# A four-layer transformer kernel: where the causal mask products stand in the transposed scores, and which head pairs run together

## The reference

```python
h = norm(x) * (1 + scale1) + shift1
x = x + gate1 * (softmax(q @ k.T / sqrt(16)) @ v @ wo + bo)     # 16 heads of 16 features
h = norm(x) * (1 + scale2) + shift2
x = x + gate2 * (act(h @ w1 + b1) @ w2 + b2)                    # 1024 hidden features
```

## Time and profile before

| | |
|---|---|
| median of 3 runs | 2475.57 us (2473.37 to 2478.87) |
| profiled execution, its own time | 2480.4 us |
| its span | 2478.5 us |
| TensorE busy | 2306.8 us (93%), 20776 products |
| VectorE, ScalarE, GpSimd busy | 66%, 51%, 44% |
| mean granted clock of TensorE | 0.982 |

### The profile page before, as it was taken

The page is one execution under the profiler, slowest core; times in us unless marked ns, Lnnn a source line. Parts: engine busy times, 40 slices in busy tenths (PEclk is TensorE's granted clock), DMA queues, the critical chain, the costliest instruction groups (busy, mean ns, idle before and its releaser), DMA issues.

```text
span 2478.5 us, 63608 instructions
## 1 busy us (share of the span) xinstructions
PE 2306.8 (93%) x20776; PEld 1908.5 (77%) x20776; DVE 1646.9 (66%) x3820; ACT 1255.5 (51%) x2624; POOL 1084.0 (44%) x1319
## 2 busy tenths in 40 slices
PE   6699999999999999999999999999999999999997
PEld 5477778877778778877777777777778787887876
DVE  3566676666665565556766676667777777677763
ACT  0366655566655554555666655566543433434332
POOL 1244444544544444444554444445534344343433
PEclk9799999999999999999999999999999999999988
DMA  6222121122211211122222211122221111111110
GB/s 211 84 67 69 63 61 61 59 71 80 90 63 57 66 59 51 61 69 78 86 79 67 68 57 58 60 70 84 64 82 45 63 51 50 65 42 60 52 53 14
DMA packets 165535, 166.66 MB, mean 67 GB/s; under 512 B 29392, under 2 KB 144976, under 8 KB 165424
## 3 DMA queue, kind: packets, MB, share of 16 engines
q1 hardware_dynamic: 165424, 165.21, 20.8%
HBM read 58.99 MB, written 4.39 MB: 26 GB/s over the span
## 4 chain that ended last, share of the span: by engine, by line
PE 47%; issue 20%; POOL 15%; DVE 10%; ACT 3%; SPq 1%; POOLq 1%; DMA 0%; DVEq 0%; ACTq 0%
PE B L481 20%; POOL GHl L1244 7%; PE B L581 7%; PE B L724 4%; PE B L530 4%; PE B L747 4%; PE B L506 3%; ACT PR L905 3%; DVE NEGM L976 2%; PE B L590 2%; POOL H1l L1283 2%; POOL X L1230 2%; POOL H2l L1270 1%; POOL X L1238 1%; PE B L600 1%
## 5 line engine op out<-in xcount | busy, mean ns | idle before, releaser
L905 ACT ACTIVATE PR<-B 128x512 f32<-128x512 f32 (+1 forms) x1024 | 508.4, 564 | 433.7 <-PE B L724 329.0
L1244 POOL TENSOR_TENSOR GHl<-G,GHh 128x256 fp32r<-128x256 f32 x512 | 376.5, 736 | 503.0 <-ACT GHh L878 332.1
L976 DVE TENSOR_REDUCE NEGM<-B 128x2 f32<-128x512 f32 x768 | 479.0, 683 | 78.7 <-PE B L530 78.0
L481 PE MATMUL B<-H2h,W1h 128*128 128x256 f32 x1280 | 394.5, 308 | 5.1 <-issue 3.1
L878 ACT ACTIVATE G<-B,VEC 128x256 f32<-128x256 f32 x384 | 182.1, 474 | 359.0 <-PE B L481 355.6
L481 PE MATMUL B<-H2h,W1l 128*128 128x256 f32 x1280 | 362.8, 283 | 0.0
L481 PE MATMUL B<-H2l,W1h 128*128 128x256 f32 x1280 | 362.3, 283 | 0.0
L747 PE MATMUL B<-PR,V 128*32 128x256 f32 (+1 forms) x4096 | 270.2, 383 | 62.8 <-ACT PR L905 62.1
L581 PE MATMUL B<-W2h,GHh 128*128 128x256 f32 x1024 | 299.2, 292 | 5.9 <-POOL GHl L1244 5.7
L581 PE MATMUL B<-W2l,GHh 128*128 128x256 f32 x1024 | 289.5, 283 | 0.0
L581 PE MATMUL B<-W2h,GHl 128*128 128x256 f32 x1024 | 288.7, 282 | 0.0
(11 more groups left out here) (140 smaller groups left out, 4977.1 us busy)
## 6 DMA issues: line engine op xcount, KB each, us to landing
QS<-QHL SPq DMA_DIRECT2D x768, 64.0 KB, 2.1
KS<-KHL SPq DMA_DIRECT2D x768, 64.0 KB, 2.1
GA<-gate_scratch SPq DMA_DIRECT2D x48, 256.0 KB, 3.1
GM<-gate_scratch SPq DMA_DIRECT2D x48, 256.0 KB, 3.4
RAW<-in_w SPq DMA_DIRECT2D x36, 256.0 KB, 3.9
CW<-in_cw SPq DMA_DIRECT2D x3, 1536.0 KB, 13.8
X<-in_x SPq DMA_DIRECT2D x2, 2048.0 KB, 10.2
QS<-MT SPq DMA_DIRECT2D x256, 4.0 KB
```

What stands on the lines that cost most here:

```text
L481: last = nc.tensor.matmul(dst, w[i], x[j], start=(first_k and n == 0), stop=(last_k and n == 2))
L905: nc.scalar.activation(PR[:, h % PRING].rearrange("p k q -> p (k q)")[:, 0:n], src[:, 0:n], ACT.Exp, scale=SCALE).then_inc(ac_exp, 1)
L976: last = nc.vector.tensor_reduce(NEGM[:, :, c], src, op=ALU.max, axis=AX.X, negate=True)
L1244: nc.gpsimd.tensor_tensor(GH[1][:, j % RING, :], G[:, j % RING, :], GH[0][:, j % RING, :].bitcast(F32), ALU.subtract).then_inc(po_gl, 1)
```

## The change

The mask product may now lead: it opens the accumulation in its bank (`start=True`) and the score products add to it. A new tuple `MASK_LEADS = (0, 3, 5, 6)` names the groups for which this holds. A new function takes one or more pairs, waits for the banks of all of them, then (in the causal layer, if the group leads) runs all their mask products, and then their score products. Outside `rope` pairs 0 and 1 are one group; in every step pairs 6 and 7 are one group. Where the mask leads, `pe_st` is raised by the product for k = 1.

```diff
+MASK_LEADS = (0, 3, 5, 6)
...
-                def mask(transposed, n):
+                def mask(transposed, n, leads=False):
...
-                    return nc.tensor.matmul(dst, IDENTB[:], MASK[:, transposed], start=False, stop=True,
+                    return nc.tensor.matmul(dst, IDENTB[:], MASK[:, transposed], start=leads, stop=not leads,
                                             skip_group_check=True)
...
-                def transposed_pair(p):
+                def transposed_pairs(*ps):
+
+                    for p in ps:
+                        banks_free(p)
+                    leads = ps[0] in MASK_LEADS
+                    if s.la == CAUSAL and leads:
+                        for p in ps:
+                            for h in (2 * p, 2 * p + 1):
+                                mask(1, ST_BANKS[rope][h], True)
+                    for p in ps:
+                        transposed_pair(p, leads)
+
+                def banks_free(p):
...
+                def transposed_pair(p, leads):
...
                             last = nc.tensor.matmul(B[:, banks[h], k * T:k * T + T - first], KS[b:b + ROWS, p, k * P:(k + 1) * P],
-                                                    QS[b:b + ROWS, p, first:T], start=(k == 0 or s.la != CAUSAL),
-                                                    stop=(s.la != CAUSAL), skip_group_check=(s.la == CAUSAL))
-                            if s.la != CAUSAL and k == NT - 1:
+                                                    QS[b:b + ROWS, p, first:T], start=(k == 0 and not leads or s.la != CAUSAL),
+                                                    stop=(leads and k == NT - 1 or s.la != CAUSAL),
+                                                    skip_group_check=(s.la == CAUSAL))
+                            if (s.la != CAUSAL or leads) and k == NT - 1:
                                 last.then_inc(pe_st, 1)
-                    if s.la == CAUSAL:
+                    if s.la == CAUSAL and not leads:
                         for h in (2 * p, 2 * p + 1):
                             mask(1, banks[h]).then_inc(pe_st, 1)
...
-                    transposed_pair(0)
-                    if not rope:
-                        transposed_pair(1)
+                    if rope:
+                        transposed_pairs(0)
+                    else:
+                        transposed_pairs(0, 1)
...
-                    transposed_pair(6)
-                    transposed_pair(7)
+                    transposed_pairs(6, 7)
```

More of the change, by code:

```diff
@@ L719, in transposed_pair @@
                             at_least(pe, dv_k, s.q_done)
+                def transposed_pair(p, leads):
+                    a_, banks = s.a, ST_BANKS[rope]
                     for k in range(NT):
@@ L808, in body @@
                 if s.a is not None:
-                    transposed_pair(0)
-                    if not rope:
-                        transposed_pair(1)
+                    if rope:
+                        transposed_pairs(0)
+                    else:
+                        transposed_pairs(0, 1)
                     maxima_to_rows(1)
                     if rope:
-                        transposed_pair(1)
+                        transposed_pairs(1)
                     if not rope:
                         values(0)
-                    transposed_pair(2)
+                    transposed_pairs(2)
                     if not rope:
                         values(1)
-                    transposed_pair(3)
+                    transposed_pairs(3)
                     outputs(0)
-                    transposed_pair(4)
+                    transposed_pairs(4)
                     if rope:
                         values(0)
-                        transposed_pair(5)
+                        transposed_pairs(5)
                         values(1)
```

## The result

The changed kernel is slower. In the first comparison its median is 2488.43 us (2484.45 to 2492.45, 5 runs) against 2473.37 us (2470.27 to 2478.87, 5 runs), ratio 1.0051, 95% interval 1.0035 to 1.0067. In a second, longer comparison it is 2488.38 us (12 runs) against 2476.19 us (25 runs), ratio 1.0045, interval 1.0029 to 1.0062. In microseconds the first is a loss of 13, between 9 and 17, the second a loss of 11, between 7 and 15. The prediction said 2483.6 from 2475.6, a loss of 8.0, range 2477 to 2490.

A forecast was written before the change was run, and what follows sets the result against it. Attention tails in layers 0 and 2 were taken as set by exponential 11, pair 6, four exponentials, outputs(3), next MLP. Layer 0 +6.1, layer 2 +3.5, causal -1.6 sum to +8.0: 2475.6 becomes 2483.6 us, range 2477 to 2490.

The forecast's parts named there:

- pair 6's wait in layers 0 and 2: Attention tail: pair 6 needs exponential 11 instead of 9; +0.28 us a step in layer 0, +0.23 in layer 2.
- rival 1: Causal layer: masks gain nothing, a mask behind a full-array product pays 0.21; sum +13.0, 2488.6 us; chance 0.13.
- Pair 0 waits for the maximum of head 14: Layer 0 tail start: pair 0 starts 0.27 us later, the MT copy moves by +0.10 a step.
- norm_2's wait: Layer 2: norm_2 waits 0.53 us for TOK on VectorE, untouched by the change, so pair 0's delay is absorbed.
- The leading masks: Causal layer, 16 steps: fewer array re-divisions gain 0.32 up to norm_2; net -0.10 us a step, -1.6 in sum.
- the stall of up(1): Causal tail: up(1) stalls 0.27 us on the copy VT, which takes up outputs(3) coming 0.16 later.
- Layer 3: Pairs 6 and 7: exponential 11 ends before pair 6 starts anyway, so joining them costs nothing.
- 2: Causal layer gains in full, pair 6's group not late; causal part -5.1, sum +4.5, 2480.1 us; chance 0.10.
- 3 (GpSimd sets the next step): Next step not started by outputs(3), so pair 6's wait is free in layers 0 and 2; -3.5, 2472.1 us; chance 0.14.
- 4 (the clock falls in the longer idle tail): Layers 0 and 2: more idle could start slow-clock stretches as in layer 3; 34 us, 2517; chance 0.05.

The follow-up runs named there:

- the one-wait kernel: Changed kernel with the group of pairs 6 and 7 waiting once, for exponential 11 alone; steps of 33.65 (layer 0), 35.69 (causal) and 34.54 us (layer 2).
- The kernel with the pairs apart: Changed kernel with pairs 6 and 7 as two groups again; steps of 33.35, 35.57 and 34.30 us, ratio to the kernel before 0.9995.
- the one with the wait alone: Kernel before with only pair 6 waiting for pair 7's banks too, masks trailing; median 2486.66 us, ratio 1.0035 to the kernel before.

## Why the prediction was right, and where it was off

The mechanism that decides, pair 6's wait in layers 0 and 2, was right. That the parts add up to so near a sum is partly luck: by steps, layer 0 gave +5.2 us from step 2 on (6.1 predicted for all 16), the causal layer -0.8 (-1.6), layer 2 +4.1 (3.5). And by the total alone rival 1, with 2488.6, looks better than the forecast; only the rows rule it out.

1. **Pair 6 waits for exponential 11: right, and it decides.** Predicted +0.28 and +0.23 a step; measured, as ScalarE's idle time before exponential 12, 0.39 to 0.73 (+0.34) in layer 0 and 0.43 to 0.73 (+0.30) in layer 2. The size was off because the group's start was taken 0.05 behind exponential 11, from a place with one wait; with two waits in a row it is 0.14 to 0.15, as the one-wait kernel shows. Of the 0.09 missed, 0.03 came back between pair 6 and exponential 12.
2. **Pair 0 waits for the maximum of head 14: wrong, a term of 0.10 that is 0.** The steps that failed are two. I put 0.15 between VectorE and TensorE, from up(1); the maximum of head 14 ends at 330.18 (0.60 ahead of head 15's, at 328.90 + 1.88 = 330.78), and pair 0 starts 0.06 behind it. So it was 0.17 late, not 0.27 (0.38 behind the last key product instead of 0.21). And the MT copy did not move: 1.49 us behind the last key product (331.35 - 329.86) against 1.48 before (326.64 - 325.16). I had its transposes hang on pair 1. They also wait for the maximum of head 15, and start 0.13 behind that in both kernels (326.23 behind 326.09, 330.91 behind 330.78). From pair 0 to the transposes there were 0.86 us before and are 0.67 now: that slack took up the 0.17. ScalarE had room too: MT stood 0.65 behind exponential 0, with 0.15 to spare over the 0.50 that now separates them. Errors 1 and 2 cancelled in part in layer 0, by luck: 0.38 predicted, 0.32 measured. In layer 2, where I had let norm_2's wait absorb the 0.10, only error 1 is left: 0.23 predicted, 0.30 measured.
3. **The leading masks: right.** Group 0, 1: 1.29 predicted, 1.26 measured. The mask behind a full-array product, which no row of before showed, costs 0.12 as taken; rival 1's 0.21 is excluded. The net in the causal layer: -0.10 predicted, -0.11 measured in the middle steps (not in the first and the last, so that the sum is half), for the reason given: outputs(3) late by the wait, the stall of up(1) gone. The kernel with the pairs apart shows the 0.32 that the wait costs there too, and the one with the wait alone shows the stall taking it up.
4. **Layer 3: right.** The wait is met anyway: exponential 11 ends at 2163.29 + 1.09 = 2164.38, pair 6 starts at 2165.53 without idle time in front of it. The steps of the trace are no longer.

```profile
2165.53 0.73 PE L740 MATMUL B<-QS,KS 64*128 64x256 f32 x8
...
2163.29 1.09 ACT L922 ACTIVATE PR<-B 128x512 f32<-128x512 f32 x2 [0.46 <-PE B L740]
```

5. **The rivals.** 2 asked for a causal gain of 0.32: it needs the pairs apart. 3 (GpSimd sets the next step) would have left layers 0 and 2 nearly as they were; they lost 0.3 each. 4 (the clock falls in the longer idle tail) did not occur: the granted clock of the changed kernel is 1.00 from 139 to 1700 us, as before, and the steps of layer 3 are not slower.
6. **The sum.** Predicted +8.0; the steps from 2 to 46 show +8.5. The timed runs show +11 (7 to 15), which holds both, and +13 (9 to 17) in the first comparison, which holds neither 8.0 nor, by a hair, 8.5. The first two steps add some (their tails grew too, by 0.8 and 0.2 us from first to last exponential), and what lies outside of the compared steps varies by more than the difference.

## What to carry to other kernels

A group that waits for the buffers of its last member before its first starts is a new dependency for the first, and it costs in every stage that takes the same code, also in those that the group was not made for: look for the latest buffer in each of them. Leading masks and joined pairs paid where the buffers had long been free, and took time where they were freed by the engine that the group feeds. When two sides join at the next step, a gain counts on the side that is waited for, and a loss only beyond the other side's lead: read the joint's stall first.

## What the runs showed of the hardware

- Going from products on the full array to a pair in halves cost 0.09 us more than going on with full ones, at a granted clock of 1.00 (0.21 against 0.12; behind two masks 0.32 against 0.23). What the way back costs by itself no run separates. Step times moved by about as much with each such change saved or added (0.06, 0.13, and 0.18 for two). A bf16 product on the full array cost nothing extra behind another full one: 0.12.
- A product behind two waits in a row on one semaphore, of which the second is the late one, started 0.14 to 0.15 us after the release, behind one wait 0.05. In steps 3 to 45 of three profiles it was 0.14 or 0.15 each time with two waits and 0.05 or 0.06 each time with one.
- Thirteen executions of kernels that are nearly the same in layer 3 differed by 7.6 us over its 16 steps, and by 11.3 us up to the end of step 1. That is more than this change is worth; only the step times told the parts apart.
